# FFN entry rebuilt in an adaLN + scan + FP4-FFN kernel, and three PSUM banks in turn for kv and a

## The reference, cut to what matters

```python
# x: (2, 4096, 512) f32; six rows sa, ca, ga, sb, cb, gb of modulation per batch from silu(c) @ wmod
h = layernorm(x) * (1 + ca) + sa
xn = h / norm(h) * sqrt(512) * gamma
q, kv, a = split(xn @ W_qkva.T)                 # W_qkva is 1536 x 512
y[t] = sigmoid(a[t]) * y[t-1] + kv[t]           # a scan along the 4096 tokens
x = x + ga * (q * y)
h = layernorm(x) * (1 + cb) + sb
# fp4_linear: blocks of 16 are scaled by max/6 and rounded to 0, .5, 1, 1.5, 2, 3, 4, 6, inputs and weights alike
u = silu(fp4_linear(h, w_gate)) * fp4_linear(h, w_up)   # 512 -> 1408
x = x + gb * fp4_linear(u, w_down)                      # 1408 -> 512
```

## Time and profile before

| | |
|---|---|
| median of 3 runs | 1962.49 us (1960.41 to 1964.91) |
| profiled execution, its own time | 1964.21 us |
| its span | 1962.4 us |
| granted TensorE clock, mean | 0.991 |
| PE busy | 1914.9 us, 98% of the span |
| DVE busy | 1725.8 us, 88% |
| POOL busy | 1233.3 us, 63% |
| ACT busy | 756.3 us, 39% |

### The profile page before, as it was taken

The page is one execution under the profiler, slowest core; times in us unless marked ns, Lnnn a source line. Parts: engine busy times, 40 slices in busy tenths (PEclk is TensorE's granted clock), DMA queues, the critical chain, the costliest instruction groups (busy, mean ns, idle before and its releaser), DMA issues.

```text
span 1962.4 us, 26907 instructions
## 1 busy us (share of the span) xinstructions
PE 1914.9 (98%) x9147; PEld 899.2 (46%) x9147; DVE 1725.8 (88%) x2170; ACT 756.3 (39%) x1013; POOL 1233.3 (63%) x1072
## 2 busy tenths in 40 slices
PE   8999999999969999999999999999999999999998
PEld 3344444444424444444444444444444444444444
DVE  6888787888858999999999999999999999999986
ACT  4565756666533233232323323322332332323221
POOL 1556666666445677677667767766776776776641
...
DMA packets 487299, 234.98 MB, mean 120 GB/s; under 512 B 425906, under 2 KB 425918, under 8 KB 487236
## 3 DMA queue, kind: packets, MB, share of 16 engines
...
## 4 chain that ended last, share of the span: by engine, by line
PE 70%; DMA 11%; DVE 8%; ACT 3%; issue 3%; SPq 2%; POOL 2%; ACTq 0%; DVEq 0%; POOLq 0%
PE bank L1108 44%; PE bank L1126 15%; PE bank L1130 7%; DMA arena<-arena 6%; DMA x_scratch<-arena 5%; DVE arena L1348 2%; PE bank L1039 2%; ACT arena L782 1%; SPq L449 1%; DVE arena L1333 1%; PE bank L978 1%; ACT arena L797 1%; DVE arena L1339 1%; DVE arena L1200 0%; DMA arena<-in_L_attn_x_dram 0%
## 5 line engine op out<-in xcount | busy, mean ns | idle before, releaser
L1108 PE MATMUL bank<-wgu_hi,arena 128*128 128x512 f16 (+1 forms) x3072 | 871.1, 362 | 19.8 <-DMA arena<-arena 19.4
L1108 PE MATMUL bank<-wgu_lo,arena 128*128 128x512 f16 (+1 forms) x1536 | 556.1, 362 | 0.0
L1039 PE MATMUL bank<-arena,wq_hi 128*128 128x512 f16 x1536 | 458.1, 380 | 7.0 <-DVE arena L1333 7.0
L1108 PEld LDWEIGHTS bank<-wgu_hi,arena 128*128 128x128 f16 x3072 | 301.0, 98 | 330.0 <-issue 23.5
L1039 PE MATMUL bank<-arena,wq_lo 128*128 128x512 f16 x768 | 291.8, 380 | 0.0
L1126 PE MATMUL bank<-wd_hi,arena 128*128 128x512 f16 x693 | 263.7, 380 | 4.4 <-DMA arena<-arena 4.4
L1126 PE MATMUL bank<-wd_lo,arena 128*128 128x512 f16 x693 | 263.7, 380 | 0.0
L1039 PEld LDWEIGHTS bank<-arena,wq_hi 128*128 128x128 f16 x1536 | 149.5, 98 | 191.3 <-DVE arena L1333 12.2
L1108 PEld LDWEIGHTS bank<-wgu_lo,arena 128*128 128x128 f16 x1536 | 150.5, 98 | 154.4 <-issue 1.1
L1442 DVE SCALAR_TENSOR_TENSOR arena<-bank,small,arena 128x512 f32<-128x512 f32 (+1 forms) x192 | 134.0, 699 | 94.2 <-PE bank L1108 94.2
L683 POOL TENSOR_TENSOR arena<-arena 128x512 f32<-128x512 f32 x63 | 153.1, 2430 | 95.4 <-DVE arena L1517 95.4
...
## 6 DMA issues: line engine op xcount, KB each, us to landing
...
arena<-x_scratch SPq DMA_DIRECT2D x128, 256.0 KB, 3.2
...
```

The costliest lines, as they stand in the source:

```text
L1039: last = pe.matmul(dst[m % 2][:, :].rearrange("p (j t) -> p j t", j=NJ), w[:, k, at], uT[p][:, half, :, k, :], start=(n == 0), stop=(n == ...
L1108: last = pe.matmul(dst[n][:, 0:w], xT[p][:, half, k, :], wt[:, k, cut], start=(m == 0), stop=(m == 3 * KD - 1))
```

## The change

Five edits:

1. **Banks.** kv and a go round three PSUM banks each from product 8 on (group 2, the third group): kv takes bank 7 too, a takes bank 6 too. The product of kv (a) then waits for scan (decay) n - 3 in place of n - 2. q keeps its two banks.
2. **Weights.** `w_normalise(w)` of slices 3 to 13 stands behind column 3 of group w, in place of behind column 2.
3. **Modulation constants.** `finish_modulation` (ten small DVE operations that the FFN's scales need) goes from group 15 to the end of group 5.
4. **Entry, first tiles earlier.** The x1 rows of tiles 0 and 1 are loaded and their `first_stats` made in group 14. In group 15 every engine's list puts tile 0 and 1 ahead: `ffn_apply` ahead of decay 1, `quantise_x(0)` ahead of mix(15, 1), `x_lo(0)` ahead of `w_lo(14)`; POOL does the adaLN of tiles 0 and 1 ahead of the last weight slice; SP turns tile 0 ahead of the last weights.
5. **Entry, tiles 2 and 3 and the last residual.** `quantise_x(2)` and (3), `x_lo(3)`, and the last group's `join_mix` and `add_x` stand in and around the chunks of tile 0, in place of behind the quantisation of its h.

```diff
-        q_bank, kv_bank, a_bank, t_bank = bank[0:2], bank[2:4], bank[4:6], bank[6:8]
+        q_bank, t_bank = bank[0:2], bank[6:8]
+        kv_banks, a_banks = (bank[2], bank[3], bank[7]), (bank[4], bank[5], bank[6])
+        TWO_BANKS = 2 * CH
...
+        def turn_of(n):
...
+return n % 2 if n < TWO_BANKS else (n - TWO_BANKS) % 3
...
+        def kv_bank(i, m):
+return kv_banks[turn_of(CH * i + m)]
...
+        def a_bank(i, m):
+return a_banks[turn_of(CH * i + m)]
...
+        def bank_free(n):
...
+return n - 1 if n < TWO_BANKS + 2 else 0 if n == TWO_BANKS + 2 else n - 2
...
-return W_AT.get(w, ((w, 2), (w + 1, 0), (w + 1, 0), (w + 1, 1), (w + 1, 1)))[step]
+return W_AT.get(w, ((w, 3), (w + 1, 0), (w + 1, 0), (w + 1, 1), (w + 1, 1)))[step]
...
     def group(i, p, b, first, last):
-        if i == NGA - 1:
...
-            sp.wait_ge(ssq_ready, NJ * NGA)
-            for t in range(2):
-                sp.dma_start(xn_in[t], x1_tile[t]).then_inc(x_in_loaded[t], 16)
...
         turn_mix(i - 1)
         if i < NGA - 1:
             turn_u(i + 1, 1 - p)
-        weight_turns(i, -1, 1)
-        if i < NGA - 1:
+            if i == NGA - 2:
+                sp.wait_ge(ssq_ready, NJ * NGA)
+                for t in range(2):
+                    sp.dma_start(xn_in[t], x1_tile[t]).then_inc(x_in_loaded[t], 16)
+            weight_turns(i, -1, 1)
             load_group(i + 3)
         else:
             for t in range(2):
                 load_normalised(t + 2, t)
+            turn_x(0, 0)
+            weight_turns(i, -1, 1)
...
         sp.wait_ge(x1_ready, NJ * i)
         sp.dma_start(x1_group[i - 1], xr).then_inc(x1_stored, 16)
+        if i == NGA - 1:
+            turn_x(1, 1)
         sp.wait_ge(x1_stored, 16 * i)
         sp.dma_start(xr, x_group[i]).then_inc(xr_loaded, 16)
         weight_turns(i, 2, 3)
...
     groups(group)
-    turn_x(0, 0)
+    turn_mix(NGA - 1)
     load_normalised(4, 0)
-    turn_x(1, 1)
-    turn_mix(NGA - 1)
-    for t in range(-1, 3):
+    turn_x(2, 0)
+    load_normalised(5, 1)
+    load_residual(0, 0)
+    turn_x(3, 1)
+    turn_h(0, 0)
+    load_normalised(6, 0)
+    load_residual(1, 1)
+    sp.wait_ge(x1_ready, NJ * NGA)
+    sp.dma_start(x1_group[NGA - 1], xr).then_inc(x1_stored, 16)
+    for t in range(1, 3):
         slot(t, t % 2)
-        if t == 0:
-            sp.wait_ge(x1_ready, NJ * NGA)
-            sp.dma_start(x1_group[NGA - 1], xr).then_inc(x1_stored, 16)
...
         for w in weights_near(i):
-            if weight_at(w, ROUND)[0] == i:
+            if weight_at(w, ROUND)[0] == i and w < NW - 1:
                 w_scales(w)
                 w_dequantise(w)
...
     for i in range(2):
         ffn_shifts(i, i)
         ffn_adaln(i, i, 0)
+    w_scales(NW - 1)
+    w_dequantise(NW - 1)
     for i in range(2):
         xq(i, i, 0)
-        ffn_shifts(i + 2, i)
-        ffn_adaln(i + 2, i, 0)
+    for i in range(2, 4):
+        ffn_shifts(i, i - 2)
+        ffn_adaln(i, i - 2, 0)
     xq(2, 0, 0)
+    xq(3, 1, 0)
 
...
         decays(i, 0)
         weights(-1)
         if not more:
-            weights(0)
+            ffn_apply(0, 0)
+            ffn_apply(1, 1)
             decays(i, 1)
+            steps_of_x(0, 0)
             split_mix(i, 0)
             join_mix(i - 1, (0, 1))
-            ffn_apply(0, 0)
-            ffn_apply(1, 1)
+            x_hi(0, 0)
+            weights(0)
             decays(i, 2)
             join_mix(i - 1, (2, 3))
             split_mix(i, 1)
-            steps_of_x(0, 0)
-            x_hi(0, 0)
+            steps_of_x(1, 1)
             ffn_apply(2, 0)
             decays(i, 3)
             split_mix(i, 2)
-            steps_of_x(1, 1)
             x_hi(1, 1)
             ffn_apply(3, 1)
...
     groups(group)
     split_mix(NGA - 1, 3)
+    steps_of_x(2, 0)
     silu(0, 0, 0, 0)
-    steps_of_x(2, 0)
+    x_hi(2, 0)
+    steps_of_x(3, 1)
     silu(0, 0, 0, 1)
-    x_hi(2, 0)
+    join_mix(NGA - 1, (0, 1))
+    x_hi(3, 1)
 
...
         if b == 0 and first:
             silu(0, 0, 0, 2)
+            join_mix(NGA - 1, (2, 3))
             steps_of_h(0, 0)
             ffn_apply(4, 0)
             silu(1, 1, 0, 0)
-            act.wait_ge(mixT_loaded, 16 * NGA)
             h_hi(0, 0)
-            steps_of_x(3, 1)
-            x_hi(3, 1)
-            join_mix(NGA - 1, range(NJ))
...
-        wait(pe, decay_ready, CH * i + m - 1)
-        product(i, p, m, 2, a_bank, a_ready)
+        wait(pe, decay_ready, bank_free(CH * i + m))
+        if CH * i + m == TWO_BANKS + 2:
...
-        wait(pe, state_ready, CH * i + m - 1)
-        product(i, p, m, 1, kv_bank, kv_ready)
+        wait(pe, state_ready, bank_free(CH * i + m))
+        product(i, p, m, 1, kv_bank(i, m), kv_ready)
...
         weights(-1)
         mix(i, p, b, 0, first)
         if not more:
-            first_stats(0)
-            first_stats(1)
+            quantise_x(0, 0)
+            mix(i, p, b, 1, first)
+            x_lo(0, 0)
             weights(0)
-            finish_modulation()
-            mix(i, p, b, 1, first)
             add_x(i - 1, (0, 1))
-            quantise_x(0, 0)
+            normalise_x(1, 1)
             mix(i, p, b, 2, first)
+            round_x(1, 1)
             add_x(i - 1, (2, 3))
             first_stats(2)
-            x_lo(0, 0)
-            quantise_x(1, 1)
-            mix(i, p, b, 3, first)
             x_lo(1, 1)
             first_stats(3)
+            mix(i, p, b, 3, first)
             return
...
         mix(i, p, b, 3, first)
+        if i == 5:
+            finish_modulation()
+        if i == NGA - 2:
+            first_stats(0)
+            first_stats(1)
         weights(3)
...
+    quantise_x(2, 0)
     hidden(0, 0, 0, 0)
-    quantise_x(2, 0)
+    x_lo(2, 0)
+    normalise_x(3, 1)
     hidden(0, 0, 0, 1)
-    x_lo(2, 0)
+    round_x(3, 1)
+    add_x(NGA - 1, (0, 1))
+    x_lo(3, 1)
...
             h_y(0, 0)
-            x_max(3, 1)
-            x_scale(3, 1)
-            x_recip(3, 1)
+            add_x(NGA - 1, (2, 3))
             h_magic(0, 0)
             h_round(0, 0)
             h_quantised(0, 0)
-            x_y(3, 1)
             hidden(1, 1, 0, 0)
             h_lo(0, 0)
-            x_magic(3, 1)
-            x_round(3, 1)
-            x_lo(3, 1)
-            add_x(NGA - 1, range(NJ))
```

More of the change, by code:

```diff
@@ L455, in load_group, with turn_x @@
                         sp.dma_start(xs[i % 2], x_group[i]).then_inc(xs_loaded[i % 2], 16)
+                def turn_x(i, p):
+                    sp.wait_ge(x_lo_ready, i + 1)
+                    sp.nop(nofuse=True)
+                    wait(sp, up_ready, NC * (i - 1))
+                    sp.nop(nofuse=True)
+                    sp.dma_start(xT[p].rearrange("p h k t -> p (h k) t"), x_half[p].rearrange("p h d -> p (h d)"),
+                                 transpose=True).then_inc(xT_loaded[p], 16)
                 def group(i, p, b, first, last):
-                    if i == NGA - 1:
-                        sp.wait_ge(ssq_ready, NJ * NGA)
-                        for t in range(2):
-                            sp.dma_start(xn_in[t], x1_tile[t]).then_inc(x_in_loaded[t], 16)
                     if i == 0:
@@ L484, in group @@
                     weight_turns(i, 2, 3)
-                def turn_x(i, p):
-                    sp.wait_ge(x_lo_ready, i + 1)
-                    sp.nop(nofuse=True)
-                    wait(sp, up_ready, NC * (i - 1))
-                    sp.nop(nofuse=True)
-                    sp.dma_start(xT[p].rearrange("p h k t -> p (h k) t"), x_half[p].rearrange("p h d -> p (h d)"),
-                                 transpose=True).then_inc(xT_loaded[p], 16)
                 def turn_h(i, p):
@@ L765, in decays @@
                     wait(act, mix_split, CH * i + m - 1)
-                    act.activation(decay[m % 2], a_bank[m % 2][:, :], ACT.Sigmoid,
+                    act.activation(decay[m % 2], a_bank(i, m)[:, :], ACT.Sigmoid,
                                    scale=col("qkva_scale")).then_inc(decay_ready, 1)
@@ L1038, in product @@
                         for w, half in ((wq_hi, 0), (wq_hi, 1), (wq_lo, 0)):
-                            last = pe.matmul(dst[m % 2][:, :].rearrange("p (j t) -> p j t", j=NJ), w[:, k, at],
+                            last = pe.matmul(dst[:, :].rearrange("p (j t) -> p j t", j=NJ), w[:, k, at],
                                              uT[p][:, half, :, k, :],
@@ L1048, in product_a @@
                         wait_uT(pe, i)
[L1049 to L1050 removed]
+                    wait(pe, decay_ready, bank_free(CH * i + m))
+                    if CH * i + m == TWO_BANKS + 2:
+                        pe.wait_ge(wk_ready, 1)
+                    product(i, p, m, 2, a_bank(i, m), a_ready)
                 def product_kv(i, p, m):
[L1053 to L1054 removed]
+                    wait(pe, state_ready, bank_free(CH * i + m))
+                    product(i, p, m, 1, kv_bank(i, m), kv_ready)
                 def product_q(i, p, m):
```

(13 more changed lines are left out.)

2 lines of the change are left out of this document (removed).

## The result

| | before | after |
|---|---|---|
| median | 1963.16 us (4 runs, 1960.41 to 1964.91) | 1951.59 us (4 runs, 1950.28 to 1953.55) |
| profiled execution, its span | 1964.21, 1962.4 us | 1950.28, 1948.5 us |
| granted clock, mean | 0.991 | 0.996 |

The ratio is 0.9943, 95% interval 0.9927 to 0.9959: 11.6 us faster by the medians, 13.9 by the two profiled executions (that of the changed kernel is the fastest of its four). The forecast was 1943, with 1935 to 1953 as the range.

A forecast was written before the change was run, and what follows sets the result against it. PE's waits, set by DVE's chain at the FFN entry, were taken as the bound: 1964.2 - 15.0 (chunk 0 of tile 2 earlier) - 4.4 (down(1)) = 1944.8 us profiled, 1943 as median. The range was 1935 to 1953.

The forecast's parts named there:

- cases 1 and 2: Case 1: the forecast as summed, 1943 us, own range 1937 to 1951, chance 0.66; Case 2 has its own line.
- down(1): PE's wait of 4.4 us at down(1), for tile 1's h, would be gone.
- Edit 1 at zero: Third banks: most of PE's 7.0 us of scan waits go, covered by its wait at the FFN entry; costed at zero.
- Edit 2, 4.5 us: From group 13, the mix ahead of w_normalise: u_lo starts 4.5 us earlier, mix(14, 3) ends at 531.5; earlier groups cost nothing.
- Edit 3, 4.2 us off the entry: finish_modulation's 4.2 us leave DVE's work at the FFN entry; in group 5 waits for ACT cover them.
- Edit 4, 36.3 us to mix(15, 3): DVE from mix(14, 3) to mix(15, 3): 25.6 us of work with gaps plus 10.7 of new waits, ending at 567.8.
- Edit 5, 28.0 us to hidden(1, 0): DVE from mix(15, 3) to hidden(1, 0): 23.8 us plus 4.2 of new waits, ending at 595.8.
- case 6: Rival: DVE blocked behind POOL's passes (shared port lock) for nearly all of them at the FFN entry; up to 1975, chance 0.02.
- Case 2: Rival: the wait only moves, DVE operations stretch beside POOL (10 us) or tile 1's h is late; 1951 to 1958.6, chance 0.13.
- Case 3: Rival: more gain, half of the 14.9 us of new waits don't occur; 1936, down to 1930, chance 0.08.
- case 4: Rival: no change, FFN entry as late as before, at most finish_modulation's 4.2 us saved; 1958.6 to 1966, chance 0.06.
- Case 5: Rival: slower, the moved mix and finish_modulation delay u_lo and PE in eleven groups, 26 us; 1969, chance 0.05.

The follow-up runs named there:

- e1: The kernel before with only the third PSUM banks for kv and a added: 1962.77 us, ratio 0.9999 to the kernel before.
- e2: The changed kernel with the third banks undone (two banks throughout): 1954.32 us, ratio 0.9955 to the kernel before.
- e5: The kernel before with only w_normalise of slices 3 to 13 moved behind column 3: 1958.37 us, ratio 0.9976 to the kernel before.
- e3: The changed kernel with w_normalise of slices 3 to 13 back ahead of the mix of column 3: 1958.09 us, ratio 0.9975 to the kernel before.
- e4: The changed kernel with finish_modulation back in group 15, ahead of quantise_x(0): 1953.23 us, ratio 0.9947 to the kernel before.
- e11: The kernel before with only w_normalise moved behind column 3 and finish_modulation moved to group 5: 1958.84 us, ratio 0.9976 to the kernel before.
- e6: The changed kernel with ACT's silu(1, 0) ahead of ffn_apply(4) in tile 0: 1950.23 us, ratio 0.9932 to the kernel before.
- e7: The changed kernel with POOL's xq(0) ahead of w_dequantise of the last weight slice: 1951.39 us, ratio 0.9936 to the kernel before.
- e10: The changed kernel with POOL's wide passes of the FFN entry done on 32 columns only, a probe: 1942.22 us, ratio 0.9896 to the kernel before.

## Why the prediction was right, and what it mis-sized

**The number.** The median, 1951.59, is in the range and 8.6 us above the forecast of 1943, at the border of cases 1 and 2. 5.5 us of this are the profiled execution (1950.28 against 1944.8). The other 3.1 are how I went from it to the median: I took 1.7 off, since the execution of before was above its median, and that of the changed kernel is 1.3 below its own. The gain is 11.6 us of some 19.5 forecast; that the range held owes something to its width.

**What bounds the kernel.** Right: PE's start of chunk 0 of tile 2 and its wait at down(1) set the time, and DVE's chain sets the first. The 9.15 us by which that chunk starts earlier are 4.9 up to mix(14, 3) and 4.3 in the entry.

**Edit 1 at zero.** Right on the old kernel (e1, ratio 0.9999), and at the entry of the changed one (e2); what the 2.7 us between the medians of e2 and the changed kernel are is open. My reason held half: of the 7.0 us most came back as waits for the mix and for u, and little had to be covered.

**Edit 2, 4.5 us.** The size is right: counted from the end of add_x of group 13 the edit is worth 4.8 us in the old kernel (e5) and 5.5 in the changed one (e3). That the end of mix(14, 3) was met within 0.4 us is in part luck. u_lo started at 509.55, 2.2 us before the 511.7 that I laid out: add_x of group 13 ended 1.2 us earlier than in the trace before, and w_normalise took 4.2 us, not the 5.2 that it takes there. A wait of 2.13 us for w_hi behind it, which I hadn't, gave that back. Its cost of nothing in the earlier groups held, but not for my reason alone. u_lo's 44 operations between 145 and 500 us grew from 0.79 to 1.19 us each, 17.6 us in all, and DVE's waits for w_hi fell from 37.7 us to 27.1; the waits covered that too.

**Edit 3, 4.2 us off the entry.** Mis-sized: it shortens the entry by 0.8 us in the changed kernel (e4) and by 1.2 in the old one (e11 against e5), where the medians show nothing. Most of what it took off DVE came back as waits for ACT and POOL.

**Edit 4, 36.3 us to mix(15, 3); 39.75 measured.** The waits sum to 10.7 us (1.58, 1.25, 2.92, 0.57, 4.36) where I laid out 10.7, but not the same ones: that the sums agree is luck. x_lo(0)'s limiter was POOL's xq(0) behind w_dequantise, not the transposes of turn_mix, whose split ran at 542.7; and quantise_x(0) had a wait of 1.58 us for adaLN that I had not. The work failed: 28.5 us and not 24.8. Of the 3.7, 2.3 are DVE standing still beside POOL (x_round 0.95, add_x 0.87, x_lo 0.48), and 1.4 are an omission of mine: x_lo(1) and first_stats(3) now stand ahead of mix(15, 3); I took them out of the second stretch and did not put them into the first. (x_magic(1), which stood still for 0.5 us before, does no more, and finish_modulation is 3.9 us of busy time, not 4.2; the two nearly cancel.)

**Edit 5, 28.0 us to hidden(1, 0); 30.6 measured.** Waits 4.8 in place of 4.2, the last of them 1.50 for silu behind ffn_apply(4), which e6 took away, and 0.6 of small gaps, which I had left out here. Again 2.6 us of DVE standing still (x_scale 0.81, x_y 0.75, add_x 0.87 and 0.13). The rest of the work is 1.1 less than I had: the 20.6 us that I took over from before held an x_y(3) that stood still for 1.1 us.

**So the step that failed** is the price of DVE beside POOL. I added nothing for it to the sum; the measured price is 4.9 us, against 1.6 in the work that the sum took over from before, so 3.3 of the 6.0 us by which the entry is longer than forecast. The next largest piece is the omission of 1.4. I had the price beside the sum as ten operations by 0.5 us, which made 1948; seven are long, by 0.13 to 0.95 us. In the entry before, only two were: POOL's passes fell mostly on scans and waits there. The new order of POOL and DVE put them on x_round, add_x and x_y.

**It was in the trace before.** I read rows 9 as 0.5 us on each add_x, and held that against case 6. But POOL's adaLN pass beside them (270.46, 1.63 us) ended at 272.09 and the second add_x at 272.65: the first took its own time, and the second stood still to the end of the pass. And in 59 tiles of the FFN x_lo took 1.75 to 1.77 us in place of 0.69, each ending 0.54 to 0.56 us behind a pass of POOL, as here (DVE, then POOL):

```profile
656.68 1.76 DVE L1435 TENSOR_TENSOR arena<-arena 128x512 f16<-128x512 f32 x1
```

```profile
655.35 2.54 POOL L654 TENSOR_TENSOR arena<-arena,sbb 128x512 f32<-128x512 f32 x1
```

There it costs nothing, since PE is the bottleneck. In the entry, where DVE is, it could have been priced pass by pass.

**down(1).** Right: no wait, 4.4 us. e3 shows its share: without edit 2 chunk 0 of tile 2 starts only 1.4 us earlier than before, and the kernel is still 0.25% faster, 4.9 us.

**Rivals.** Case 2 (only moved, through stretched operations) was in part what came: its mechanism, 4.9 us of its 10. Case 3 fell, since the new waits came in full (15.5 us of 14.9), and so did case 4, since chunk 0 of tile 2 starts 9.15 us earlier. Case 5 is refuted as a total. Case 6 had the right mechanism, as e7 and e10 show, and the wrong extent: DVE stood still for 4.9 of POOL's 36 us busy, since mostly it was waiting anyway, or in a scan, mix or hidden, which POOL didn't slow.
